# State-space scan of a four-layer-kind transformer kernel: the input B·(dt·x) built by ScalarE and TensorE instead of VectorE, the C rows loaded by DMA, and ScalarE scaling the rows of the next unit's normalisation

## What is computed

```python
x = silu(conv(x)); x_dbl = x @ W_x
dt = softplus(x_dbl[..., :64] @ W_dt + b_dt)
Bm, Cm = x_dbl[..., 64:80], x_dbl[..., 80:]
A = -exp(A_log)                                  # 256 channels x 16 states
def step(h, inp):
    dA = exp(dt_t[..., None] * A)
    h = dA * h + (dt_t * x_t)[..., None] * B_t[:, None, :]
    y = einsum('bdn,bn->bd', h, C_t)
```

## Time and profile before

| | |
|---|---|
| Median of 3 runs | 1458.77 us (1455.15 to 1463.09) |
| Profiled execution: its time / its span | 1453.59 / 1451.8 us |
| Mean granted PE clock in it | 0.937 of 2.4 GHz |
| PE busy / DVE / ACT / POOL | 84% / 69% / 41% / 17% |

### The profile page before, as it was taken

One profiled execution on the slowest core, in us unless ns is written; L12 is line 12 of the kernel. 1 busy time (PEld: TensorE's weight loads), 2 busy tenths in 40 slices (PEclk: granted clock), 3 DMA queues, 4 the chain that ended last, 5 costly groups with the idle time before them and its releaser, 6 DMA issues.

```text
span 1451.8 us, 16322 instructions
## 1 busy us (share of the span) xinstructions
PE 1221.3 (84%) x5704; PEld 746.4 (51%) x5704; DVE 1001.1 (69%) x1944; ACT 596.5 (41%) x995; POOL 242.7 (17%) x211
## 2 busy tenths in 40 slices
PE   5997888999997565769999977889989966757798
PEld 3675444676664222236667644446766622312565
DVE  6666665555685996977764776655556779789665
ACT  4543455344225345422234424554432254455222
POOL 3001000000200461532000010000001015436110
PEclk9999799999998697889999999999999978969899
DMA  6203120001010000010200122100010100000120
GB/s 209 58 23 103 46 61 3 1 1 44 15 59 0 1 0 0 0 59 1 66 23 1 39 64 75 32 2 0 1 59 1 58 0 0 0 0 1 58 62 12
DMA packets 27314, 45.06 MB, mean 31 GB/s; under 512 B 3648, under 2 KB 19296, under 8 KB 27040
## 3 DMA queue, kind: packets, MB, share of 16 engines
q1 hardware_dynamic: 27232, 44.02, 10.1%
HBM read 36.34 MB, written 8.19 MB: 31 GB/s over the span
## 4 chain that ended last, share of the span: by engine, by line
PE 61%; DVE 21%; issue 8%; ACT 4%; DMA 2%; POOL 1%; SPq 1%; DVEq 0%; POOLq 0%; ACTq 0%
PE bank L1403 12%; PE bank L1405 11%; PE bank L1404 11%; PE bank L1569 8%; DVE n_h L1371 4%; DVE a_mx L1307 3%; PE bank L1412 3%; PE bank L1481 3%; DVE bank L1363 3%; PE bank L1542 2%; PE bank L1628 2%; PE bank L1728 2%; DMA a_k<-stack_dram 2%; PE bank L1603 2%; PE bank L1666 1%
## 5 line engine op out<-in xcount | busy, mean ns | idle before, releaser
L1156 DVE SCALAR_TENSOR_TENSOR f_hl<-bank,f_hh 128x512 fp32r<-128x512 f32 x192 | 131.8, 689 | 129.0 <-ACT f_hh L831 128.1
L831 ACT ACTIVATE f_hh<-bank 128x512 fp32r<-128x512 f32 x192 | 114.7, 597 | 189.0 <-PE bank L1481 188.6
L765 POOL TENSOR_TENSOR n_hc<-n_h,n_cs 128x512 f32<-128x512 f32 x128 | 160.8, 1272 | 140.8 <-DVE n_h L1371 86.8
L893 ACT ACTIVATE m_sl<-bank 128x512 f32<-128x512 f32 x144 | 85.8, 597 | 220.6 <-PE bank L1405 218.5
L1403 PE MATMUL bank<-xT_h,mw_h 128*128 128x512 f32 x288 | 161.0, 559 | 7.0 <-DVEq L506 4.3
L1728 PE MATMUL bank<-n_hc,ident 128*128 128x512 f32 x256 | 151.0, 712 | 10.8 <-POOL n_hc L765 9.8
L1371 DVE TENSOR_TENSOR_SCAN n_h<-n_da,bank 128x512 f32<-128x512 f32 x128 | 149.1, 1201 | 3.6 <-POOL n_hc L765 3.6
L984 ACT ACTIVATE n_da<-n_dt,amat 128x512 f32<-128x512 f32 x128 | 91.7, 721 | 132.1 <-DVE n_h L1371 125.1
L1569 PE MATMUL bank<-m_h,mw 128*128 128x512 f32 x288 | 145.6, 594 | 0.0
L1307 DVE TENSOR_REDUCE a_mx<-bank 128x1 f32<-128x384 f32 (+3 forms) x176 | 106.2, 637 | 50.2 <-PE bank L1668 47.6
L1223 DVE TENSOR_TENSOR m_t<-m_sl,bank 128x512 f32<-128x512 f32 x128 | 87.9, 686 | 73.7 <-PE bank L1405 72.6
(11 more groups left out here) (231 smaller groups left out, 2397.2 us busy)
## 6 DMA issues: line engine op xcount, KB each, us to landing
m_c<-comb_dram SPq DMA_DIRECT2D x28, 512.0 KB, 5.1
a_q<-stack_dram SPq DMA_DIRECT2D x8, 512.0 KB, 4.7
a_k<-stack_dram SPq DMA_DIRECT2D x16, 256.0 KB, 5.2
stage_fw<-in_fw_dram SPq DMA_DIRECT2D x6, 512.0 KB, 7.6
stack_dram<-R SPq DMA_DIRECT2D x16, 192.0 KB, 2.8
w_stage<-in_mw_dram SPq DMA_DIRECT2D x9, 256.0 KB, 2.7
stack_dram<-R SPq DMA_DIRECT2D x16, 128.0 KB, 2.6
m_c0b<-comb_dram SPq DMA_DIRECT2D x4, 512.0 KB, 3.6
```

Source lines behind the costliest of these rows:

```text
L765: n_hcs.by(nc.gpsimd.tensor_tensor(n_hc[:, m, :], n_h[:, m, :], n_cs[:, n // 2 % 2, :], ALU.mult))
L831: f_hi.by(act.activation(f_h[0][:, i % 4, :], bank[:, i % 3, :], ACT.Relu))
L1156: f_lo.by(V.scalar_tensor_tensor(f_h[1][:, i % 4, :], bank[:, i % 3, :], 0.0, f_h[0][:, i % 4, :].bitcast(F32), ALU.max, ALU.subtract))
```

## The change

B is no longer broadcast. dt·x is transposed once per unit by PE (8 transposes into PSUM banks 4 and 5, tokens on partitions), where B of one state is one number per partition. ACT multiplies by it (`inputs`, four 128x256 instructions per state with a per-partition scale, from PSUM to `n_sx`), and PE turns the result back into PSUM (`n_dbs`, eight 128x128 transposes per state), where the scan reads it. B transposed comes from 8 small matmuls more in each unit (`n_btp`). C rows go to DRAM and come back broadcast over the partitions, two states per DMA, eight DMAs of 512 KB per unit into a ring of three. `n_da`, `n_h`, `n_hc` get four buffers, `drive` three banks, `n_sx` two. And in Mamba units ACT, not DVE, makes the last scaled rows of the next unit (stage "norm").

```diff
+LOOP_ACT_STAGES = {"moe": {3: "norm", 5: "high", 8: "exp 0"}, "mamba": {5: "norm", 7: "high"}}
...
+        n_da = sb("n_da", [P, 4, T], F32, s)
+        n_h = sb("n_h", [P, 4, T], F32, s)
+        n_hc = sb("n_hc", [P, 4, T], F32, s)
+        n_sx = sb("n_sx", [P, 2, NT, NHALF * P], F32, s)
+        n_cs = sb("n_cs", [P, C_RING, 2, T], F32, s)
+        n_bT = sb("n_bT", [P, NT, NSTATE], F32, s)
...
+        def dtx_rows(c):
+            return bank[:, 4 + c // 2, c % 2 * NHALF * P:(c % 2 + 1) * NHALF * P]
... SP
+            def state_rows(k):
+                sp.wait_ge(n_crs.sem, n_crs.at(k, 0))
+                n_cwr.by(sp.dma_start(c_dram, n_crow[80:96]))
+                sp.wait_ge(n_cwr.sem, n_cwr.at(k, 0))
+                for j in range(C_LOADS):
+                    if j >= C_RING:
+                        sp.wait_ge(n_hcs.sem, n_hcs.at(k, 4 * (j - C_RING) + 3))
+                    n_cld[j % C_RING].by(sp.dma_start(n_cs[:, j % C_RING],
+                                                      c_dram[2 * j:2 * j + 2].unsqueeze(0).to_broadcast([P, 2, T])))
... POOL
+                    for i in range(2 * NSTATE):
+                        pool.wait_ge(n_scan.sem, n_scan.at(k, i))
+                        j = i // 4
+                        if i % 4 == 0:
+                            pool.wait_ge(n_cld[j % C_RING].sem, n_cld[j % C_RING].at(k, j // C_RING))
+                        if i >= 4:
+                            pool.wait_ge(n_ya.sem, n_ya.at(k, i - 4))
+                        n_hcs.by(nc.gpsimd.tensor_tensor(n_hc[:, i % 4, :], n_h[:, i % 4, :],
+                                                         n_cs[:, j % C_RING, i // 2 % 2, :], ALU.mult))
... ACT
+                if stage == "norm":
+                    act.wait_ge(g_off.sem, g_off.at(kth[u - 1], 0))
+                    for t in range(NT):
+                        if kind == "moe":
+                            ins = act.activation(xn[:, p, t, :], X[:, batch_of(u), t, :], ACT.Identity,
+                                                 bias=shift[:, t:t + 1], scale=rstd[:, t:t + 1])
+                        else:
+                            ins = act.activation(xm[p][:, t, :], xn[:, p, t, :], ACT.Copy, scale=rstd[:, t:t + 1])
+                    g_xn.by(ins)
...
-                act.wait_ge(n_dts.sem, n_dts.at(k, 0))
+                for i in range(2):
+                    act.wait_ge(n_dts.sem, n_dts.at(k, i))
+                    decays(k, i)
+                act.wait_ge(n_dxt.sem, n_dxt.at(k, 0))
+                inputs(k, 0)
                 for n in range(NSTATE):
-                    for m in range(NHALF):
-                        if n >= 1:
-                            act.wait_ge(n_scan.sem, n_scan.at(k, 2 * n + m - 2))
-                        n_das.by(act.activation(n_da[:, m, :], n_dt[:, m, :], ACT.Exp, scale=amat[:, m, n:n + 1]))
-                    act.wait_ge(n_cr.sem, n_cr.at(k, n))
-                    if n >= 2:
-                        act.wait_ge(n_hcs.sem, n_hcs.at(k, 2 * n - 3))
-                    n_csc.by(act.activation(n_cs[:, n % 2, :], bank[:, 0, :], ACT.Copy))
-                    hand_over(u, n)
+                    if n + 1 < NSTATE:
+                        inputs(k, n + 1)
+                        decays(k, 2 * n + 2)
+                        decays(k, 2 * n + 3)
+                    hand_over(u, n - 1)
+            def decays(k, i):
+                if i >= 4:
+                    act.wait_ge(n_scan.sem, n_scan.at(k, i - 4))
+                n_das.by(act.activation(n_da[:, i % 4, :], n_dt[:, i % 2, :], ACT.Exp, ...))
+            def inputs(k, n):
+                if n >= 2:
+                    act.wait_ge(n_dbs.sem, n_dbs.at(k, 2 * n - 3))
+                for c in range(NT):
+                    ins = act.activation(n_sx[:, n % 2, c, :], dtx_rows(c), ACT.Copy, scale=n_bT[:, c, n:n + 1])
+                n_sxs.by(ins)
... DVE
-                for n in range(NSTATE):
-                    dve.wait_ge(n_br.sem, n_br.at(k, n))
-                    for m in range(NHALF):
-                        ...
-                        n_dbs.by(V.tensor_tensor(drive(m), n_dtx[:, m, :], bank[:, 4 + n % 2, :], ALU.mult))
-                    for m in range(NHALF):
-                        ...
-                        n_scan.by(V.tensor_tensor_scan(n_h[:, m, :], n_da[:, m, :], drive(m), 0.0,
-                                                       ALU.mult, ALU.add))
-                    hand_over(u, n)
+                for i in range(2 * NSTATE):
+                    dve.wait_ge(n_dbs.sem, n_dbs.at(k, i))
+                    dve.wait_ge(n_das.sem, n_das.at(k, i))
+                    if i >= 4:
+                        dve.wait_ge(n_hcs.sem, n_hcs.at(k, i - 4))
+                    n_scan.by(V.tensor_tensor_scan(n_h[:, i % 4, :], n_da[:, i % 4, :], drive(i), 0.0,
+                                                   ALU.mult, ALU.add))
+                    if i % 2 == 1:
+                        hand_over(u, i // 2)
... PE
+                for c in range(NT):
+                    for m in range(2):
+                        ins = mm(bank[:, 5, c * NSTATE:(c + 1) * NSTATE], n_xc[:, m, c * P:(c + 1) * P],
+                                 wx[:, m, 64:64 + NSTATE], start=m == 0, stop=m == 1)
+                n_btp.by(ins)
                 pe.wait_ge(n_dtc.sem, n_dtc.at(k, 0))
...
+                for m in range(NHALF):
+                    pe.wait_ge(n_dtxs.sem, n_dtxs.at(k, m))
+                    ins = rows(lambda t: dtx_rows(t)[:, m * P:(m + 1) * P],
+                               lambda t: n_dtx[:, m, t * P:(t + 1) * P], ident[:])
+                n_dxt.by(ins)
+                for i in range(2 * NSTATE + 4):
+                    n, m = divmod(i, NHALF)
                     if n < NSTATE:
-                        ...
+                        pe.wait_ge(n_sxs.sem, n_sxs.at(k, n))
+                        if i >= 3:
+                            pe.wait_ge(n_scan.sem, n_scan.at(k, i - 3))
+                        n_dbs.by(rows(lambda t: drive(i)[:, t * P:(t + 1) * P],
+                                      lambda t: n_sx[:, n % 2, t, m * P:(m + 1) * P], ident[:]))
+                    if i >= 4:
+                        pe.wait_ge(n_hcs.sem, n_hcs.at(k, i - 4))
+                        n_ya.by(mm(bank[:, 2 + m, :], ident[:], n_hc[:, i % 4, :], start=n == 2, stop=n == NSTATE + 1))
+                    if m == 1:
+                        hand_over(u, n - 1)
```

More of the change, by code:

```diff
@@ L26 @@
 NSTATE, NHALF = 16, 2
+C_RING, C_LOADS = 3, 8
 EPS = 1e-5
@@ L135, in stage_at @@
                 return ahead.get(i)
+    if host == "mamba" and table is ACT_STAGES:
+        return LOOP_ACT_STAGES[kind].get(i)
     if kind == "mamba":
@@ L222, in program @@
         mv = sb("mv", [P, NT, 2])
-        small = sb("small", [P, 8, NT])
-        preload, y0, ve, y2, rstd, gmax, gsum, grec = (small[:, i, :] for i in range(8))
+        small = sb("small", [P, 9, NT])
+        preload, y0, ve, y2, rstd, gmax, gsum, grec, shift = (small[:, i, :] for i in range(9))
         gbuf = sb("gbuf", [P, 6, NT, EXPERTS])
@@ L457, in program @@
         n_dtc = sig("n_dtc", "mamba", 1)
[L458 to L461, removed]
+        n_btp = sig("n_btp", "mamba", 1)
+        n_bts = sig("n_bts", "mamba", 1)
+        n_crs = sig("n_crs", "mamba", 1)
+        n_cwr = sig("n_cwr", "mamba", 1, 16)
+        n_cld = [sig(f"n_cld_{c}", "mamba", len(range(c, C_LOADS, C_RING)), 16) for c in range(C_RING)]
         n_dtp = sig("n_dtp", "mamba", 2)
@@ L497, in ffn_lag, with scaled_by_act @@
             return FFN_LAG if UNITS[u][1] == 1 else 3 * after_heads(u)
+        def scaled_by_act(u):
+            return u > 0 and UNITS[u - 1][0] == "mamba"
         def done_before(u):
@@ new lines, in mamba @@
+                act.wait_ge(n_dxt.sem, n_dxt.at(k, 0))
+                inputs(k, 0)
+                for n in range(NSTATE):
+                    if n + 1 < NSTATE:
[6 more added lines that the diff above has]
+                    act.wait_ge(n_scan.sem, n_scan.at(k, i - 4))
+                n_das.by(act.activation(n_da[:, i % 4, :], n_dt[:, i % 2, :], ACT.Exp,
+                                        scale=amat[:, i % 2, i // 2:i // 2 + 1]))
@@ L1037, in step, with newton @@
                 dve.wait_ge(dve_step, steps[0])
-            def newton():
+            def newton(last=None):
                 step(V.tensor_tensor(y2, y0, y0, ALU.mult))
@@ L1068, in prologue @@
                     newton()
+                    if scaled_by_act(u) and kind == "moe":
+                        dve.wait_ge(dve_step, steps[0])
+                        g_off.by(V.scalar_tensor_tensor(shift, mv[:, :, 0], -1.0, rstd, ALU.mult, ALU.mult))
+                        return
                     for t in range(NT):
@@ new lines, in mamba @@
+                step(V.scalar_tensor_tensor(n_cor, n_cor, 0.0, n_u, ALU.min, ALU.add))
+                for m in range(NHALF):
+                    dve.wait_ge(n_poss.sem, n_poss.at(k, m))
```

(20 more changed lines are left out.)

131 lines of the change are left out of this document (44 added, 87 removed).

## The result

The changed kernel takes 1407.2 us (median of 4 runs, 1403.9 to 1411.3), the kernel before 1460.1 beside it: ratio 0.964, 95% interval 0.961 to 0.968. That is 52 us faster (47 to 58), where 40 were predicted and 1419 us, range 1400 to 1441. The profiled execution has a span of 1402.2 us against 1451.8.

A forecast was written before the change was run, and what follows sets the result against it. The prediction took DVE to bound the four Mamba loops; 13.9 us gained per loop less 3.9 lost ahead of it gave 10 per unit, 40 in all: 1458.8 - 40 = 1419 us, range 1400 to 1441.

The forecast's parts named there:

- DVE bounds the loops before: In the four Mamba loops before the change, DVE works all the time, busy 97 to 99%; windows mean 64.4 us.
- The state costs 2.78 us on ACT: In the new loop, per state: four inputs 1.52 us and two decays 1.26, sum 2.78, bounds 2.1 and 3.3.
- rival 3: New loop: ACT gives nothing back between inputs, 3.3 us per state, 1452 us in all; chance 0.06.
- The low clock costs 2 us in the loop: First states of the new loop: PE starts at the low clock, costing 2 us per unit.
- the 4.0 of another term: Ahead of the loop: first scan 4.0 us after dt·x, for transposes, inputs, second transposes and waits; before 1.24.
- ACT sets the rhythm, the rest hides; 1 us for the long piece, 1 for meshing: New loop: ACT bounds, most hosted DVE work hides; DVE's longest piece and imperfect meshing add 1 us each; loop 50.5.
- Ahead of the loop +3.9: Before each loop: the later first scan costs 2.8 us and B transposed 1.1, together 3.9 per unit.
- B transposed: Ahead of the loop: its small matmuls hold W_dt back by 1.1 us per unit, bounds 0 and 3.
- Four buffers give more than 2 us of play: New loop: decays have 2.6 us of play, PE 2.2; shorter stalls are absorbed, hiding most hosted DVE work.
- Rival 2: New loop: about eight hosted DVE operations stretch beside POOL products, up to 10 us; DVE stays the bound, 1441; chance 0.15.
- Rival 4: New loop: PE falls to the low clock at the hosted burst, 5.3 us per state; eight such states give 1499; chance 0.06.
- Rival 5: New loop: C loads come late, a broadcast taking 8 us; 1474 us in all; chance 0.03.

The follow-up runs named there:

- e2: The kernel before with only the scaled rows moved from DVE to ACT; 1448.1 us, ratio to before 0.993.
- e8: The changed kernel with ten filling matmuls on PE between W_dt and the transposes of dt·x; 1404.7 us, ratio to before 0.962.
- e3: The changed kernel with one more 128x256 instruction on ACT per state, result unread; 1417.3 us, ratio to before 0.972.
- e4: The changed kernel with four more transposes on PE per state, work done twice; 1424.3 us, ratio to before 0.976.
- e5: The changed kernel with one more 128x256 multiplication on DVE per state, result unread; 1414.3 us, ratio to before 0.970.
- e1: The changed kernel with the scaled rows back on DVE; 1408.7 us, ratio to before 0.965.
- e6: The changed kernel with decays, scans and products in two buffers instead of four; 1484.6 us, ratio to before 1.018.

## Why the prediction was right, and where its sizes were off

*DVE bounds the loops before.* Right: e2's 2 us per unit came back on average (7.8 us in all, 7.6 expected).

*The state costs 2.78 us on ACT.* Measured 2.65, 2.1 us less per unit. The kind of sum held: an input with a per-partition operand is spaced 0.355 us, 0.38 predicted, and not the 0.47 of rival 3.

*The low clock costs 2 us in the loop.* Wrong place. Nothing was lost in the loop, as the clock had risen before the first sum; e8 shows 1.2 us ahead of the loop, inside the 4.0 of another term.

*ACT sets the rhythm, the rest hides; 1 us for the long piece, 1 for meshing.* This is the step that was half right. ACT's 2.65, with PE's 2.60, rules only in the later states; in states 0 to 4 of a mixture-hosting loop and 0 to 6 of a Mamba-hosting one DVE sets the pace, and what it hosts there is paid in full (e3, e4, e5, and e1's 0.88 us). Mamba-hosting loops, where DVE hosts more, are 2.6 us longer. With 50.5 predicted against 48.0 measured, the loop term was 2.5 us too long per unit: 2.1 the rhythm, 2.0 the clock, less 1.6 that I had too little for meshing and pieces. That two of these cancel in part is luck, and so is some of the good fit of the time: the range was right, the picture of one engine that works all the time was not.

*Ahead of the loop +3.9.* Measured 3.12 + 0.72 = 3.84. The transposes, the inputs and the second transposes add in the way worked out, 4.36 against 4.0 for the path: the first transposes end 1.5 us behind dt·x, not 1.09. B transposed costs 0.72 against 1.1. The sum fits because the two misses cancel, which is luck too.

*Four buffers give more than 2 us of play.* The play was needed, and more than the prediction said: without it everything is lost, with PE's list as it is (e6). Its size isn't shown: behind the 5.2 us piece ACT stood 3.7, so 1.5 us of play were left when it began, but DVE was late already from the statistics behind state 0. And where DVE sets the pace, absorbing its stalls for ACT shortens nothing.

*Rival 2, DVE stays the bound.* Two of the four root operations stretched, to 0.6 and 1.2 us in the first root of a unit (the 488.99 and 489.59 rows) and to 1.2 both in the second root of units 8 and 20, where one operation per root had before. That is some 2 us per root at most, and not eight operations. They end with POOL's products, at 489.54 and 490.77. By the rule of the Trainium skill that the prediction cites (SBUF — State Buffer, section "SBUF: two separate sides"), that DVE operations with two SBUF inputs and GpSimd operations exclude each other, the trace agrees. The rival was right in part: in the first third to half of the loops DVE is the bound, though not by this stretching alone. *Rival 4, the clock falls in the loop.* It does fall in units 8 and 20 behind the long piece (the sum of 1.72 us at 496.03), for two states, not for the four that would have mattered, and DVE's scans come without a gap all the while. *Rival 5.* C loads landed in 3.7 us, and no wait of POOL for one stands in the trace.

The sum: predicted -13.9 + 3.9 = -10 per unit, measured -16.65 + 3.84 = -12.8. Of the missing 2.8 the new loops are 2.5 (48.0, not 50.5), and 0.25 is that the loops before were 64.65 us, not 64.4.

## What to carry to other kernels

When the only busy engine is relieved, the pace can go to one engine in one part of a loop and to another in the next; here four engines were 82 to 94% busy, and extra work on any of ACT, PE and DVE showed by about half. An average over the loop doesn't tell which is which, the time of each state under a little added work does. Count the buffers around the circle before moving work to an engine further away: a longer circle with the old two buffers was slower than the kernel it was to replace. Hosted work is paid in full in the states in which its own engine sets the pace, so it is better placed in the others. A stall of another engine is worth removing only if somebody waits for it. And a filler that keeps an engine awake must end before its real work is ready, at the low clock too.

## What the runs showed of the hardware

- Four fp32 128x128 transposes between other matmuls take 0.44 us of PE at the full clock, eight at the low clock 1.94; the former stayed so cheap that turning 128x512 back cost PE less than the 0.59 us that the multiplication cost DVE (1.18 for two).
- An operation of 128x4 elements on DVE (0.16 us alone) lasts up to 1.2 us while POOL multiplies, ending with POOL's product; scans with one operand in PSUM don't stretch (1.20 us on average before, 1.21 after, 1.22 at most).
- 16 MB more of DMA traffic into SBUF during the loops (54 to 57 GB/s) changed no duration by more than 0.01 us on average: scans 1.20 and 1.21, POOL's products 1.27 and 1.28.
